# A transformer layer on one core: the end of batch one's attention placed behind the experts, and the last keys split ahead of the result transfers

## The reference

```
x + attention(xn) + ffn(xn)
attention: q = xn w_q, k = xn w_k (64 wide); softmax(causal(q k^T / 8)) (xn w_v1) w_v2
ffn:  logits = xn w_router^T; the one best of 16 experts for each token
      s = sigmoid(logit) on that expert, else 0
      expert: (up * silu(gate)) down, with gate, up = (s xn) gate_up_proj (2 x 256 wide)
      shared: (silu(xn w_gate^T) * (xn w_up^T)) w_down^T
```

## Time and profile before

| | |
|---|---|
| median of 3 runs | 219.84 us (219.8 to 220.07) |
| the profiled execution's own time | 219.81 us |
| its span, first to last instruction | 218.0 us |
| mean granted TensorE clock | 0.997 |
| busy PE / PEld / DVE / ACT / POOL | 203.7 / 161.6 / 150.0 / 130.1 / 136.5 us |

### The profile page before, as it was taken

How to read it: one execution, slowest core, us unless ns; L and a number is a source line. 1 busy time by engine, 2 the same in 40 slices (tenths; PEclk the granted TensorE clock), 3 DMA queues, 4 the chain that set the end, 5 groups by cost and what they waited for, 6 DMA issues and landing times.

```text
span 218.0 us, 4536 instructions
## 1 busy us (share of the span) xinstructions
PE 203.7 (93%) x1289; PEld 161.6 (74%) x1289; DVE 150.0 (69%) x352; ACT 130.1 (60%) x303; POOL 136.5 (63%) x243
## 2 busy tenths in 40 slices
PE   4998999999889999989899999999999969899994
PEld 4786878788668775564589999999999857575663
DVE  2988798789788796852276876666666655868632
ACT  2367695766648887763545555544445576876651
POOL 3475730088888898881007998989898987363000
PEclk9999999999999999999999999999999999999998
DMA  5999999701191116413452322232332107296051
GB/s 168 284 345 336 293 285 430 304 27 46 37 230 40 37 37 161 120 38 63 55 54 81 85 59 80 82 94 86 91 78 65 39 6 184 62 338 191 3 146 50
DMA packets 30263, 28.38 MB, mean 130 GB/s; under 512 B 8835, under 2 KB 26378, under 8 KB 29600
## 3 DMA queue, kind: packets, MB, share of 16 engines
q1 hardware_dynamic: 27712, 23.85, 38.7%
q0 software_dynamic: 2528, 4.24, 6.2%
HBM read 14.36 MB, written 10.50 MB: 114 GB/s over the span
## 4 chain that ended last, share of the span: by engine, by line
PE 67%; DVE 11%; POOL 7%; issue 5%; ACT 4%; DMA 4%; SPq 1%; DVEq 0%; ACTq 0%; POOLq 0%
PE acc L1532 7%; PE mid L1395 7%; PE acc L1412 7%; PE big L1204 6%; PE acc L1258 6%; PE big L1206 6%; PE big L1205 6%; POOL y_rows L485 4%; PE acc L1436 4%; PE mid L1521 4%; PE big L1379 4%; PE big L1376 3%; DMA k_raw<-qk_all 2%; DVE stats L514 2%; PE mid L1354 2%
## 5 line engine op out<-in xcount | busy, mean ns | idle before, releaser
L485 POOL DMA_INDIRECT y_rows<-y,slot_info x47 | 47.4, 1008 | 24.4 <-ACT y L1148 16.3
L459 POOL DMA_INDIRECT scratch<-rows,slot x32 | 34.1, 1065 | 19.3 <-DVE slot L710 14.2
L776 DVE TENSOR_REDUCE negmax<-big 128x1 f32<-128x128 f32 (+7 forms) x32 | 23.9, 752 | 12.1 <-PE big L1379 11.8
L1085 ACT COPY pt<-mid 128x512 f32<-128x512 f32 (+3 forms) x48 | 22.0, 480 | 14.9 <-PE mid L1395 13.3
L866 DVE COPY eht<-mid 128x512 f32<-128x512 f32 (+1 forms) x24 | 16.3, 679 | 19.2 <-PE mid L1521 19.2
L1148 ACT COPY y<-acc 128x256 f32<-128x256 f32 (+1 forms) x24 | 8.8, 368 | 33.2 <-PE acc L1532 33.2
L1532 PEld LDWEIGHTS acc<-wed,eht 128*128 128x128 f32 x188 | 24.4, 191 | 1.8
L1071 ACT ACTIVATE prob<-big,negmax 128x128 f32<-128x128 f32 (+7 forms) x32 | 23.7, 744 | 3.2 <-DVE negmax L776 2.9
L1532 PE MATMUL acc<-wed,eht 128*128 x188 | 24.9, 275 | 0.0
L1395 PEld LDWEIGHTS mid<-identf,prob 128*128 128x128 f32 x144 | 16.3, 141 | 9.1 <-issue 3.9
L1395 PE MATMUL mid<-identf,prob 128*128 128x128 f32 x144 | 22.5, 279 | 0.4 <-ACT prob L1071 0.4
(11 more groups left out here) (148 smaller groups left out, 457.9 us busy)
## 6 DMA issues: line engine op xcount, KB each, us to landing
we_raw<-w_gate_up SPq DMA_DIRECT2D x4, 1024.0 KB, 11.1
scratch<-blank SPq DMA_DIRECT2D x1, 3120.0 KB, 17.4
xe<-scratch SPq DMA_DIRECT2D x24, 130.0 KB, 2.3
q_raw<-qk_all SPq DMA_DIRECT2D x8, 256.0 KB, 4.9
k_raw<-qk_all SPq DMA_DIRECT2D x8, 256.0 KB, 5.2
wed<-w_down SPq DMA_DIRECT2D x1, 2048.0 KB, 17.1
expert_out<-y_rows SPq DMA_DIRECT2D x8, 256.0 KB, 4.5
out<-res SPq DMA_DIRECT2D x7, 256.0 KB, 2.7
```

The lines of the kernel that those rows point to most:

```text
L459: pool.indirect_dma_start(scratch, bass.IndirectOffsetOnAxis(ap=slot[:, t:t + 1], axis=0), rows[:, t, :], None).then_inc(row_sent[t % FLY] ...
L485: pool.indirect_dma_start(y_rows, bass.IndirectOffsetOnAxis(ap=slot_info[:, t, 0:1].bitcast(U32), axis=0), y[p % NY][:, t % 2, :], None, b ...
L776: dve.tensor_reduce(negmax[:, i:i + 1], buf[:, at:at + (i + 1) * P], AX.X, ALU.max, negate=True).then_inc(max_ready, 1)
```

## The change

- **Keys of batch two** (counted from zero, so the third of four): POOL makes both halves of `k_hi` and `k_lo` ahead of its loop over the results, and nothing between two transfers. `k_raw` gets a second buffer, and SP's `load_raw` of the next batch waits for the keys of the batch before the last one only. `y` has 5 buffers instead of 6, and `h_last` lies lower, to make room.
- **Attention of batch one**: steps 8 to 11 (`transposes`, `keep_pt`, `weigh`) and the output of its second group go behind the experts, between the scores of batch two. Steps 6 and 7 are weighed in the second pair of the experts, step 7 is transposed right ahead of the first. The first two `transpose_rows` stand earlier, ahead of the output of batch one's first group.
- **Front**: `rsqrt` is made four columns at a time, and ACT's `normalize` of groups 4 and 6 goes to POOL, so that POOL scales groups 3 to 7. `xt_lo(2)` stands ahead of `hidden(0, 1)`. On TensorE `rank` stands right behind `count`, and `place_experts` and `place_tokens` stand earlier on DVE.
- **DVE**: seven `weights_lo` of the stretch 43 to 66 become three; `weights_lo(8)` to `(11)` stand at 94 and later, behind the experts' names. The two halves of batch zero's key split are pulled apart.

```diff
@@ SP
-                sp.wait_ge(k_lo_ready, FIRST + 2 * b + 2)
-                load_raw((b + 1) * S)
+                sp.wait_ge(k_lo_ready, FIRST + 2 * b)
+                load_raw(b + 1)
...
-            sp.wait_ge(k_lo_ready, FIRST + 2 * (B - 2) + 2)
-            load_raw((B - 1) * S)
+            sp.wait_ge(k_lo_ready, FIRST + 2 * (B - 2))
+            load_raw(B - 1)
@@ POOL
+            def rsqrt(b, u):
+                half = slice(u * GT, (u + 1) * GT)
+                t = slice(b % 2 * BT + u * GT, b % 2 * BT + (u + 1) * GT)
+                pool.wait_ge(var_ready, b + 2 if b else u + 1)
+                pool.tensor_tensor(rstd[:, t], var[:, half], minus_half[:, half], ALU.pow).then_inc(rstd_ready, 1)
...
             for b in range(1, B):
-                rsqrt(b)
-                if b > 1:
-                    shifts(b)
-                normalize(2 * b + 1)
+                for u in range(2):
+                    rsqrt(b, u)
+                    if b > 1 or u:
+                        normalize(2 * b + u)
...
-            last_keys_hi(0, K_FIRST)
-            last_keys_lo(0, K_FIRST, 1)
+            for half in range(2):
+                last_keys_hi(half * S // 2, (half + 1) * S // 2)
+            for half in range(2):
+                last_keys_lo(half * S // 2, (half + 1) * S // 2, half + 1)
...
-                    if k_column(t) < S:
-                        last_keys_hi(k_column(t), k_column(t + 1))
-                    if t and k_column(t - 1) < S:
-                        last_keys_lo(k_column(t - 1), k_column(t), t + 1)
@@ DVE
             hidden(5, 0)
             add_shared(4)
-            split_q_lo(0, 0)
-            weights_lo(3)
-            weights_lo(4)
-            hidden(5, 1)
-            split_q_lo(0, 1)
+            split_k_lo(0, 1)
+            hidden(5, 1)
+            split_q_lo(0, 0)
+            weights_lo(1)
...
+            weights_lo(8)
             add_attention(0, 1)
-            sums(1)
-            add_attention(1, 0)
+            for e in range(9, ON_DVE):
+                weights_lo(e)
             rows_lo(0, 0)
-            keep_mixed(1, 1)
             rows_lo(1, 1)
...
                 if p == 0:
-                    add_attention(1, 1)
+                    sums(1)
+                    add_attention(1, 0)
...
-            row_max(2, 3, 4, 5, 6, 7)
+            row_max(2, 3, 4, 5)
+            keep_mixed(1, 1)
+            row_max(2, 6, 7)
+            add_attention(1, 1)
             split_k_hi(3, 0)
@@ ACT
+            keep_pt(1, 8)
             load_table(ACT.Exp)
             keep_rows(21)
             exp(2, 0, 1, 2)
             keep_rows(22)
+            keep_pt(1, 9)
             exp(2, 3)
             keep_rows(23)
-            exp(2, 4)
-            keep_pt(2, 0)
-            exp(2, 5)
-            keep_pt(2, 1)
+            keep_pt(1, 10, 11)
+            exp(2, 4, 5)
+            keep_pt(2, 0, 1)
@@ PE
-            weigh(1, 2, 3)
-            transposes(1, 5, 6)
+            weigh(1, 2)
+            transposes(1, 5)
+            weigh(1, 3)
+            transposes(1, 6)
+            transpose_rows(0, 0)
+            weigh(1, 4, 5)
+            transpose_rows(1, 1)
             outputs(1, 0)
             transposes(1, 7)
-            weigh(1, 4, 5)
-            transposes(1, 8)
-            weigh(1, 6)
-            transposes(1, 9)
-            weigh(1, 7, 8)
-            transposes(1, 10)
-            transpose_rows(0, 0)
-            weigh(1, 9)
-            transposes(1, 11)
-            weigh(1, 10, 11)
-            transpose_rows(1, 1)
...
-                if p == 0:
-                    outputs(1, 1)
+                if p == 1:
+                    weigh(1, LATER - 1, LATER)
...
+            transposes(1, 8)
             scores(2, 0, 1)
             transpose_hidden(NP - 2, 0)
...
             down(NP - 2, 0, e_before)
+            transposes(1, 9)
             scores(2, 4)
+            transposes(1, 10)
             _, e_before = ahead.pop()
             down(NP - 1, 1, e_before)
+            transposes(1, 11)
             scores(2, 5)
-            transposes(2, 0)
+            weigh(1, 8, 9, 10, 11)
             scores(2, 6)
-            transposes(2, 1)
+            transposes(2, 0, 1)
             scores(2, 7)
-            transposes(2, 2, 3)
+            transposes(2, 2)
+            outputs(1, 1)
+            transposes(2, 3)
             weigh(2, 0, 1, 2, 3)
@@ sizes
-NY = 6
+NY = 5
-K_FIRST, K_PIECE = 304, 18
+LATER = 7
```

More of the change, by code:

```diff
@@ L132, in build @@
         q_hl = sb("q_hl", [P, S], F32R)
-        k_raw = sb("k_raw", [P, S])
+        k_raw = [sb(f"k_raw{n}", [P, S]) for n in range(2)]
         k_hi, k_lo = sb("k_hi", [P, S], F32R), sb("k_lo", [P, S], F32R)
@@ L161, in build @@
         y, y_end = overlay(c_end, [(f"y{q}", [P, 2, P], F32) for q in range(NY)])
-        h_last, last_end = overlay(max(a_end, b_end), [(f"h_last{c}", [P, GC], F32) for c in range(FC)])
+        h_last, last_end = overlay(max(a_end - hot_size, c_end), [(f"h_last{c}", [P, GC], F32) for c in range(FC)])
         assert d_end <= rows_end
@@ L463, in last_keys_hi @@
             def last_keys_hi(first, stop):
-                pool.tensor_copy(k_hi[:, first:stop], k_raw[:, first:stop]).then_inc(k_hi_pieces, 1)
+                pool.tensor_copy(k_hi[:, first:stop], k_raw[0][:, first:stop]).then_inc(k_hi_pieces, 1)
             def last_keys_lo(first, stop, n):
                 pool.wait_ge(k_hi_pieces, n)
-                last = pool.tensor_tensor(k_lo[:, first:stop], k_raw[:, first:stop],
+                last = pool.tensor_tensor(k_lo[:, first:stop], k_raw[0][:, first:stop],
                                           k_hi[:, first:stop].bitcast(F32), ALU.subtract)
-                if first < S // 2 <= stop or stop == S:
-                    last.then_inc(k_lo_ready, 1)
-            def k_column(n):
-                return K_FIRST + n * K_PIECE
+                last.then_inc(k_lo_ready, 1)
             pool.wait_ge(raw_ready, 64 * (B - 1))
             pool.wait_ge(s_done, FIRST + (B - 2) * BT)
-            last_keys_hi(0, K_FIRST)
-            last_keys_lo(0, K_FIRST, 1)
+            for half in range(2):
+                last_keys_hi(half * S // 2, (half + 1) * S // 2)
+            for half in range(2):
+                last_keys_lo(half * S // 2, (half + 1) * S // 2, half + 1)
             for p in range(NP):
@@ L631, in _ @@
             batch_statistics(2)
+            xt_lo(2)
             hidden(0, 1)
-            xt_lo(2)
             batch_statistics(3)
@@ L672, in split_k_hi @@
                 dve.wait_ge(s_done, FIRST + b * BT)
-                dve.tensor_copy(k_hi[:, cols], k_raw[:, cols]).then_inc(k_hi_ready, 1)
+                dve.tensor_copy(k_hi[:, cols], k_raw[b % 2][:, cols]).then_inc(k_hi_ready, 1)
             def split_k_lo(b, half):
@@ L677, in split_k_lo @@
                 dve.wait_ge(k_hi_ready, 2 * (b if b < B - 2 else b - 1) + half + 1)
-                dve.tensor_tensor(k_lo[:, cols], k_raw[:, cols], k_hi[:, cols].bitcast(F32), ALU.subtract
+                dve.tensor_tensor(k_lo[:, cols], k_raw[b % 2][:, cols], k_hi[:, cols].bitcast(F32), ALU.subtract
                                   ).then_inc(k_lo_ready, 1)
@@ L735, in _ @@
             sum_tiles(1)
+            place_experts()
             hidden(2, 0)
-            place_experts()
             to_score()
+            place_tokens()
             hidden(2, 1)
+            xt_lo(5)
             add_shared(1)
-            xt_lo(5)
-            place_tokens()
             hidden(3, 0)
@@ L825, in _ @@
             hidden(NG - 1, 0)
-            weights_lo(7)
+            weights_lo(3)
             hidden(NG - 1, 1)
             row_max(0, 0, 1)
-            weights_lo(8)
+            weights_lo(4)
             row_max(0, 2, 3)
-            weights_lo(9)
+            weights_lo(5)
             row_max(0, 4)
-            weights_lo(10)
+            weights_lo(6)
             row_max(0, 5)
@@ L845, in _ @@
             row_max(1, 1, 2)
-            weights_lo(11)
+            weights_lo(7)
             split_q_lo(1, 1)
@@ L940, in xt_hi @@
                 act.copy(xth[g % XB][:, :], qk_all[:, g * GC:(g + 1) * GC]).then_inc(xth_ready[u], 1)
-            def normalize(g):
-                b, u = g // 2, g % 2
-                act.wait_ge(shift_ready, b - 1)
-                for t in range(GT):
-                    n = b % 2 * BT + u * GT + t
-                    act.activation(flat(rows[:, g * GT + t:g * GT + t + 1, 0:P]),
-                                   flat(res[:, g * GT + t:g * GT + t + 1, :]), ACT.Identity,
-                                   bias=shift[:, n:n + 1], scale=rstd[:, n:n + 1]).then_inc(xn_ready[u], 1)
             def keep_logits(g):
@@ L1300, in _ @@
             project_logits(7)
+            gate_up(2, 1)
+            project_qk(4)
             down(1)
-            gate_up(2, 1)
             def count():
@@ L1317, in rank @@
                           ).then_inc(ranked, 1)
```

(5 more changed lines are left out.)

50 lines of the change are left out of this document (16 added, 34 removed).

## The result

The changed kernel takes 222.64 us in the median of 20 runs (219.5 to 225.35), the kernel before 219.91 us in 20 runs beside them (219.6 to 220.49). The ratio is 1.0084, with a 95% interval of 1.0066 to 1.0102: **slower**, clear of noise though by under 2%, where 217.9 was forecast. The spread is part of the result: the kernel before runs at a mean granted clock of 0.997 in its profile, the runs of the changed one at 0.969 to 0.991, but for one at 1.0, and that one took 219.5. The ratio leaves out the seven runs of the changed kernel that lie over 1.5% above its fastest, so that the medians stand further apart (1.012) than it says. The profiled run took 221.2 us, with a span of 219.4 us at a clock of 0.984.

What follows compares the result with a forecast made beforehand. TensorE's gaps were taken as the bound: waits for keys behind the experts and gaps ahead of them. 219.81 - 2.7 (ahead of the experts) + 0.8 (behind, waits removed included) = 217.9 us; range 215.9 to 219.8.

Steps and rivals of the forecast that it cites:

- What bounded the kernel: TensorE's gaps: waits behind the experts from key pieces between POOL's transfers, and gaps of some 1.7 us at 96 to 107.
- Keys ahead of the loop: Splitting batch two's keys before POOL's results loop removes TensorE's waits at and after batch two's scores, together 2.7 us.
- The front at nothing, covered: At the start, TensorE falls 1.9 us behind but is level again at 96, waiting for rows; cost nothing.
- The sum: Whole kernel: 219.81 - 2.7 + 0.8 = 217.9 us, with the first rows landing at 100.7.
- Ahead of the experts: Rows land at 100.7, 3.45 us of TensorE work follows, experts begin at 104.2 instead of 106.86: -2.7 us.
- Behind the experts: Between experts and batch three's scores: 3.6 us of work in, 2.7 of waiting out; +0.8, between +0.4 and +1.7.
- the collision that the upper bound named: Behind the experts, POOL's adds of returned results run beside the key splits and slow them; one collision makes +1.7 us.
- the clock: TensorE's 4.4 us gap at 96 lowers its clock, costing 2.3 to 3.5 us; about 220.9 us, chance 0.12.

Runs made afterwards that it cites:

- experiment 3: Kernel before with only all keys of batch two split ahead of the results; median 217.69 us, ratio 0.9901.
- experiment 7: Kernel before with all keys of batch two ahead of the results and the changed front, steps 8 to 11 unmoved; median 219.85 us, ratio 0.9983.
- experiment 9: Kernel before with all keys ahead of the results and VectorE's new order of weight splits, old front, steps 8 to 11 unmoved; median 216.86 us, ratio 0.9851.
- experiment 1: Changed kernel with 26 unused transposes filling TensorE's idle stretch ahead of the first rows; median 219.13 us, ratio 0.9943.
- experiment 8: Changed kernel with 13 unused transposes in the idle stretch ahead of the first rows; median 217.95 us, ratio 0.9896.
- experiment 4: Kernel before with only steps 8 to 11 of batch one and their additions moved behind the experts; median 223.63 us, ratio 1.0157.
- experiment 10: Changed kernel with the front of the kernel before; median 223.94 us, ratio 1.0089.
- 11: Changed kernel with the old front, steps 8 and 9 ahead of the rows, batch three's key split ahead of the last addition; median 217.62 us, ratio 0.9887.
- 6: Changed kernel with 26 unused transposes in the gap and batch three's key split ahead of the last addition of attention; median 218.15 us, ratio 0.9906.
- 12: Changed kernel with the idle stretch filled by its own work, last addition of attention ahead of batch three's key split; median 217.21 us, ratio 0.9895.

## Why the prediction was wrong

- *What bounded the kernel*: right. The waits put down to the keys between the transfers went with them.
- *Keys ahead of the loop*, 2.7 us: right in kind, 2.26 by itself (experiment 3). The last q and k load at 165.5 and the last transfer of results at 182.6 came as forecast.
- *The front at nothing, covered*: TensorE's delay, 1.9 us, was covered as forecast; uncovered it costs 2.16 (experiment 7). That the VectorE order gives it back (experiments 7 and 9) was right too. Missed: the two together move the landing of the rows, 100.44 in the changed kernel and 102.38 with the old front. The sum had 100.7, and that it was right for the kernel that was forecast is luck in part. It took 0.6 us (of a worked out 0.7) for pieces and transfers that meet fewer `weights_lo`. With VectorE's order alone (experiment 9) the pieces took 521 ns in the mean instead of 451, and the last transfer of rows started at 97.81 instead of 96.56; with the front alone (experiment 7) at 97.14. Only both together gave 95.63, with the longest piece behind the last transfer.
- *Ahead of the experts*, the experts at 104.2 for -2.7 us: **the step that failed**. It held the 3.45 us of work behind the gap at the durations of the earlier trace rows, and they hold for a TensorE that hasn't stood still: in the changed kernel this work took 5.02 us (100.44 to 105.46) and in the filled one 3.29 (100.61 to 103.90). The gap was 3.31 us, not 4.4: TensorE came to it at 97.13 and not at 96.2 (the earlier trace rows give 96.4 for the kernel before), and that was enough for the clock to fall. With the stretch filled the experts begin at 103.90 and their last product is 2.65 us earlier than before, as the sum had it; unfilled, that gain is lost, with 1.56 us gone by the experts' start and 1.35 in their first six products and the transposes round them.
- *Behind the experts*, +0.8 with bounds of +0.4 to +1.7: from the experts' last product to batch three's first score it was 17.1 us instead of 16.1, where the sum had 16.9, with the collision that the upper bound named. The same order of work took 16.3 us there in experiment 8 and 18.2 in experiment 1, each in one trace.
- *The rivals*: the clock, at 0.12, is what happened. Its price of 2.3 to 3.5 us was right for the profiled run (2.9). The argument that kept its chance low, a gap of 3.2 us of which the trace "shows no case in its middle", was no evidence, for no gap as long as that stands there at all, with a fallen clock or without. What was there, twenty transposes at 0.227 us each behind 3.15 us of idling, pointed the other way. It is weaker evidence than the prediction made of it: the granted clock of the same trace reads 1.00 from 3 to 8 us, so that the durations alone speak for the lower level.

The Trainium skill says of this on its page "TensorE: Matmul & The Clock Gate", in "Part 1: The HAM clock gate (the "warmup" mystery)", that the throttled state is the default and that activity releases it. The runs here agree: in the middle of the kernel, in experiments 4, 10 and 11 and in the changed kernel, the clock is at half its level behind an idle stretch. On the collision its page "SBUF — State Buffer", section "Who interferes with whom", says that a cast on VectorE can take the port pair that it shares with GpSimd. The trace agrees, with the cast at 1.27 to 1.50 us beside an addition on GpSimd and 0.42 alone.

If the forecast had taken the clock as the likeliest case, its own figure of 220.9 us would have been near the profiled 221.2, and the median of 222.64 still higher.

**Left open.** Why the changed kernel's runs spread from 219.5 to 225.35, when experiment 4, with a longer gap, doesn't; one trace for each kernel can't show it. Whether the three runs of experiments 6, 8 and 12 at a clock under 0.993 had the second idle stretch of experiment 1. And whether the order of the addition is worth anything beside the filled stretch.

## What to carry to other kernels

When work is moved away from in front of a wait for a transfer, look at what the waiting engine does meanwhile, not only at when it goes on: where TensorE stood still for 2.6 us or more ahead of the experts, the work right behind it ran at half its rate, and with 3.3 and 4.3 us the move cost more than it brought. Put independent work of its own ahead of the wait; it may be exactly the work that stands behind it. Then compare with the kernel that doesn't move the work: here experiment 9 did as well without. And time the parts of a change one by one: this one held a part worth 2.3 us, a part worth 0.8 more, and one that lost 3.7.

## What was new on the hardware

- TensorE's clock against its idle time ahead of the experts, each from one trace: with idle stretches of 1.05 us (experiment 9) and 1.96 us (8) it stayed at 1.00. With 2.64 us (11) it was 0.68 and 0.75 in the 3 us stretches from 101 and 104; with 3.31 us (changed kernel) 0.76 over 96 to 107 and down until 108; with 4.27 us (4) 0.89 in 96 to 101, inside the wait, and 0.50 from 101 until 110; with 7.53 us (10) already 0.68 in 96 to 101, still inside the wait, and 0.50 until 110.
- The same at batch three's first score: waits of 1.40 us (changed kernel) and 2.26 us (experiment 10, at 194.73) left the clock at 1.00, and 2.48 us (experiment 1) was followed by 0.50 in 190 to 194.
- The price isn't the same from run to run: one program took 219.5 to 225.35 us. Its time followed its mean clock only roughly: ten runs at 0.977 took 222.48 to 225.15.
- Thirteen transposes whose result nobody reads made the kernel 4.7 us faster in the median.
- A piece of 64 columns on GpSimd, 0.33 us alone, took 1.66 us beside three `weights_lo` in a row, in the kernels with VectorE's new order; whether it fell ahead of the last transfer of rows made 1.3 us of a difference of 2.1 in when that transfer started.
